# Causal attention of a two-layer block: value products on quarters of the TensorE array, score products on quarter rows two heads at a time, and other weights for its place beside the grouped attention

## The chip, the cores and the metric

The kernel runs on one core of a Trainium2 chip. The metric is the device time of one execution in microseconds, the median of three runs. Engines: TensorE (PE; PEld is its weight load), VectorE (DVE), ScalarE (ACT), GpSimd (POOL), SyncE (SP, which issues transfers).

## What is computed

Eight batch elements of 512 rows and 128 channels pass through two layers, each modulated by a small table. Layer 0: linear attention with 16 heads and an MLP (`attn0`), then 8 dense experts with a SiLU gate (`experts`). Layer 1: causal softmax attention with 8 heads of 16 channels (`attn1`), then a grouped attention with 16 heads of 64 channels, whose values are mixed and whose outputs are masked by top-2 gates over 8 experts (`gates`, `values`, `heads`). The change is in the causal attention. The reference in short, its shapes scaled up by the input (8 elements, T = 512, H = 8, HD = 16):

```python
qkv = (x @ Wqkv).reshape(b, t, 3, H, HD)
q, k, v = ...
scores = einsum('bhqd,bhkd->bhqk', q, k) * scale
scores = scores + head_scales * geo_bias
scores = where(causal, scores, -inf)
attn = softmax(scores, axis=-1)
out = einsum('bhqk,bhkd->bhqd', attn, v)
return out.reshape(b, t, d) @ Wout
```

The geometric bias is folded into the query weights once, in the setup.

## The kernel before, in words

Everything is float32 and lies in SBUF for one element at a time; matmul results go to eight PSUM banks of 512 columns: F0 to F3 for everything but the grouped attention, S0, S1 (scores), TB and OB for that one. Each engine has its own program, written as generators per stage that wait on semaphores. A stage's generator yields marks. `schedule` takes a list of main marks and a list of marks beside them, and runs the second evenly among the first, by weight: `weight(name, m)` is 1 for most marks, and for the marks of the causal attention it was (i+1)/4, with i the query tile. All engines follow the same order of marks, so it fixes each queue.

The steady loop, for element b: `heads(b-1)`, 83 steps of the grouped attention of the element before, with `attn1(b)`, `gates(b)`, and of the next element `load`, `attn0` and `moe_in` beside them; then `experts(b+1)` with the end of `heads(b-1)` and `values(b)` beside them. Element 0's causal attention has nothing beside it. Element 7's is beside `heads(6)`, with its gates and 24 marks of its values behind it.

The causal attention of an element (`attn1`): ScalarE copies the queries, transposed (channel by row), to `q1T` (a name for `attT`); the keys, transposed, go to `k1T`; `k1z[:, h, :]` is `k1T` with all channels but those of head h set to zero, made for heads 0 to 3 by ScalarE (L1142) and for heads 4 to 7 by GpSimd (L690). Then 32 head steps n = 8 i + h over query tile i (128 rows) and head h. The key width is w = 128 (i+1).
- TensorE, at mark n: the score of n (L892: the contraction over all 128 channels, of which 16 count) and the causal mask by a bf16 matmul on top (L893), in F0 or F2 by turns; the transposes of the probabilities of n-2 into F3 (L740); the value product of n-3 (L908), for each key tile with the transposed probabilities as the weights and 17 columns of `v1` (16 channels and a column of ones, which gives the denominator) streaming.
- VectorE: the negated maximum of n (L1451); after each query tile a copy of F1 to `o1` (L1445).
- ScalarE: the copy of the transposed probabilities of n-2 to `p1T` (L1149), the exponential of n (L1155).
`p1`, `p1T` and `nmax1` have two buffers each. At the end the division (L1456, L1458), a transpose and the output projection (L919).

The grouped attention in `steps`: score pairs on the two row halves (L1023), maximum (L1571), exponential (L1240), transposes (L740) and their copy (L1227), value products on the two column halves (L1060); `queries`, `back`, `mixed` and `result` are further kinds of step (L1014, L1027 with L1565, L1035, L1041).

## Time and profile before

| | us |
|---|---|
| median of three runs | 2946.02 |
| lowest and highest | 2940.43, 2952.31 |
| the profiled execution | 2954.08 |
| its span, first to last instruction | 2952.4 |
| TensorE busy | 2493.8 |
| VectorE busy | 1553.8 |
| ScalarE busy | 1360.1 |
| GpSimd busy | 803.0 |
| mean granted TensorE clock | 0.932 |

The rows further down are from the profiled execution, and so are all durations. One turn of the steady loop is some 350 us. Matmul records show how long one takes from first column to last result, and they overlap: the pace is read from when the next one starts.

### The profile page before, as it was taken

The numbers are of one execution on the slowest core, as the hardware profiler recorded it, in microseconds if no ns is written. First come the engines' busy times: TensorE is split into PE (matmuls) and PEld (weight loads), VectorE is DVE, ScalarE is ACT, GpSimd is POOL, SyncE is SP. The second block draws the span as 40 slices with busy tenths as digits, with TensorE's granted clock in tenths as the row PEclk, the third lists the DMA queues.
The fourth block names the chain that finished last, engine by engine and source line by source line (L and its number), as shares of the span: only waits on it lengthen the run. The fifth ranks groups of instructions, "written<-read, shape, count | busy, mean of one in ns | idle before, by whom it ended". The sixth has DMA issues, their size and how long they took to land.

```text
span 2952.4 us, 41528 instructions
## 1 busy us (share of the span) xinstructions
PE 2493.8 (84%) x15660; PEld 1540.7 (52%) x15660; DVE 1553.8 (53%) x2640; ACT 1360.1 (46%) x2923; POOL 803.0 (27%) x376
## 2 busy tenths in 40 slices
PE   4886799889897898978988898978989789886787
PEld 2354346554475445654466544754456544664455
DVE  3224683456635475364844457354753648446732
ACT  0232236463364625555265633646255552653364
POOL 0000560015600183012800147001740129004500
PEclk7887799999999999999999999999999999997799
DMA  2110110202010030101201121010301012000101
GB/s 77 39 55 1 29 44 1 58 15 69 22 29 31 15 87 4 44 15 47 58 1 44 30 58 33 11 49 15 80 12 44 15 43 62 1 15 18 37 23 40
DMA packets 210688, 101.15 MB, mean 34 GB/s; under 512 B 137367, under 2 KB 189620, under 8 KB 210492
## 3 DMA queue, kind: packets, MB, share of 16 engines
q1 hardware_dynamic: 205052, 95.74, 11.7%
q10 hardware_dynamic: 5440, 2.75, 0.3%
q8 instruction: 128, 2.10, 0.3%
q14 instruction: 68, 0.56, 0.1%
HBM read 77.48 MB, written 20.99 MB: 33 GB/s over the span
## 4 chain that ended last, share of the span: by engine, by line
PE 54%; ACT 10%; DVE 9%; issue 9%; POOL 4%; DMA 0%; DVEq 0%; POOLq 0%; ACTq 0%
PE bank L740 11%; PE bank L1023 10%; PE bank L1060 7%; PE bank L892 4%; POOL prod L725 4%; PE bank L855 3%; PE bank L852 3%; PE bank L908 3%; PE bank L860 3%; ACT pr L1240 3%; ACT prT L1227 3%; DVE prod L1524 2%; PE bank L1035 2%; PE bank L1014 2%; DVE nmax L1571 1%
## 5 line engine op out<-in xcount | busy, mean ns | idle before, releaser
L725 POOL TENSOR_TENSOR prod<-pv,mixv 128x1024 f32<-128x1024 f32 x190 | 609.8, 3253 | 251.3 <-ACT pv L1187 173.6
L1571 DVE TENSOR_REDUCE nmax<-bank 128x1 f32<-128x512 f32 x512 | 340.9, 686 | 541.0 <-PE bank L1023 540.6
L1227 ACT ACTIVATE prT<-bank 128x512 f32<-128x512 f32 x512 | 305.7, 597 | 609.9 <-PE bank L740 605.7
L1023 PE MATMUL bank<-keys,qs 64*128 64x512 f32 x896 | 278.4, 695 | 184.7 <-ACT pr L1240 67.2
L664 POOL TENSOR_TENSOR rstd<-vareps,minus_half 128x4 f32<-128x4 f32 x48 | 48.4, 1009 | 1272.2 <-DVE vareps L1334 1272.2
L1240 ACT ACTIVATE pr<-bank,nmax 128x512 f32<-128x512 f32 x512 | 350.3, 686 | 68.2 <-DVE nmax L1571 66.9
L740 PEld LDWEIGHTS bank<-ident,pr 128*128 128x128 f32 x2048 | 240.1, 149 | 265.5 <-issue 252.6
L740 PE MATMUL bank<-ident,pr 128*128 128x128 f32 x2048 | 347.0, 296 | 33.4 <-ACT prT L1227 32.5
L1127 ACT ACTIVATE arena<-bank 128x512 f32<-128x512 f32 x256 | 152.9, 597 | 473.8 <-PE bank L852 425.9
L1060 PE MATMUL bank<-prT,vals 128*64 128x128 f32 x3584 | 264.9, 293 | 51.4 <-ACT prT L1227 51.4
L1532 DVE TENSOR_REDUCE vals<-prod 128x128 f32<-128x1024 f32 x224 | 269.1, 1208 | 41.9 <-POOL prod L725 41.9
L1423 DVE TENSOR_TENSOR arena<-bank,arena 128x512 f32<-128x512 f32 x256 | 174.9, 685 | 214.8 <-PE bank L855 191.7
L855 PE MATMUL bank<-h1T,Wu 128*128 128x512 f32 x512 | 268.6, 607 | 20.1 <-DVE arena L1423 20.1
L1451 DVE TENSOR_REDUCE nmax<-bank 128x1 f32<-128x128 f32 (+3 forms) x256 | 125.8, 492 | 289.1 <-PE bank L893 288.5
L852 PE MATMUL bank<-h1T,Wg 128*128 128x512 f32 x512 | 267.1, 603 | 2.2 <-ACT h1T L1092 2.2
L860 PE MATMUL bank<-arena,Wd 128*128 128x512 f32 x512 | 263.7, 600 | 2.8 <-DVE arena L1423 2.3
L1060 PEld LDWEIGHTS bank<-prT,vals 128*64 128x64 f32 x3584 | 209.3, 146 | 97.0 <-issue 69.3
L892 PE MATMUL bank<-arena,attT 128*128 128x512 f32 (+3 forms) x512 | 202.1, 480 | 4.7 <-ACT arena L1155 3.2
L1023 PEld LDWEIGHTS bank<-keys,qs 64*128 64x128 f32 x896 | 76.1, 196 | 237.0 <-issue 103.1
L1524 DVE TENSOR_TENSOR prod<-pv,mixv 128x1024 f32<-128x1024 f32 x66 | 181.6, 2752 | 0.0
L855 PEld LDWEIGHTS bank<-h1T,Wu 128*128 128x128 f32 x512 | 97.6, 193 | 149.9 <-issue 112.2
L1149 ACT ACTIVATE arena<-bank 128x128 f32<-128x128 f32 (+3 forms) x256 | 112.1, 438 | 124.2 <-PE bank L740 123.4
(231 smaller groups left out, 3272.7 us busy)
## 6 DMA issues: line engine op xcount, KB each, us to landing
Wg<-in_L_ffn_Wg SPq DMA_DIRECT2D x64, 256.0 KB, 2.7
Wu<-in_L_ffn_Wu SPq DMA_DIRECT2D x64, 256.0 KB, 3.1
Wd<-in_L_ffn_Wd SPq DMA_DIRECT2D x64, 256.0 KB, 3.7
out_rows<-on SPq DMA_DIRECT2D x32, 512.0 KB, 2.6
onR<-out_rows SPq DMA_DIRECT2D x32, 512.0 KB, 3.8
xin<-in_L_attn_x SPq DMA_DIRECT2D x8, 256.0 KB, 4.3
mask_rows<-masko SPq DMA_DIRECT2D x8, 256.0 KB, 4.3
maskR<-mask_rows SPq DMA_DIRECT2D x8, 256.0 KB, 6.8
```

Source lines behind the costliest of these rows:

```text
L725: g.tensor_tensor(*value_piece(n), ALU.mult).then_inc(vprod_r[0], 1)
L740: last = pe.transpose(dst[:, i * P:(i + 1) * P], src(i), ident[:, :])
L852: pe.matmul(F0[:, :], Wg[:, e % 2, j * P:(j + 1) * P], hbT[:, :], start=True, stop=True).then_inc(gu_g[0], 1)
L855: pe.matmul((F2, F3)[n % 2][:, :], Wu[:, e % 2, j * P:(j + 1) * P], hbT[:, :], start=True, stop=True).then_inc(gu_u[0], 1)
L860: pe.matmul(F1[:, :], Wd[:, e % 2, j, :], act[:, m % 3, :], start=(m == 0), stop=(m == n_all - 1)).then_inc(down_ps[0], 1)
L892: pe.matmul(f[:, 0:w], q1T[:, i * P:(i + 1) * P], k1z[:, h, 0:w], start=True, stop=False, skip_group_check=True)
L1023: pe.matmul(S[(turn + odd) % len(S)][:, :], qs[half, j % 3, r, :], keys[half, p, :], start=True, stop=True).then_inc(s_ps[0], 1)
L1060: last = pe.matmul(OB[DS * odd:DS * odd + DS, at:at + P], vals[:, j, h - 1 + odd, :], prT[:, (m - 1 + odd) % 3, j * P:(j + 1) * P], start= ...
L1227: s.activation(prT[:, m % 3, :], TP[m % len(TP)][:, :], ACT.Copy).then_inc(pT_r[0], 1)
L1240: s.activation(pr[:, x % NPR, :], bank_k[:, :], ACT.Exp, bias=nmax[:, x % NPR:x % NPR + 1], accum_out=den[:, i % 2, h:h + 1]).then_inc(s_o ...
L1532: v.tensor_reduce(vals[:, i, HQ * q:HQ * q + HQ, :], prod[:, m % NPROD, :].rearrange("p (h d e) -> p h d e", h=HQ, e=NE), X_AXIS, ALU.add) ...
L1571: v.tensor_reduce(nmax[:, m % NPR:m % NPR + 1], S[turn % len(S)][:, :], X_AXIS, ALU.max, negate=True).then_inc(nmax_r[0], 1)
```

## The change

- **Keys.** `k1z` has two tiles instead of eight: the keys times `parity`, whose column 0 is one on the channels of even heads and column 1 on those of odd heads (made once in the setup). VectorE writes both from PSUM. `k1T`, and the masking on ScalarE and GpSimd, are gone.
- **Scores.** A head's score contracts only over the 32 channels (partitions) of its pair of heads, of which `parity` leaves 16. Heads are taken in `ORDER1`, so that two successive ones lie on different 32 partitions, and both scores are issued one behind the other at even n, into F0 and F2, then both masks.
- **Maxima and exponentials.** VectorE does both maxima of such a pair at the even mark, ScalarE both exponentials. `p1` and `nmax1` have four buffers.
- **Values.** Four heads together (`QUAD`): `v1`, padded with zeros to 32 columns per head (`DV`), is the weight, and the transposed probabilities stream, 128 columns each. The four outputs lie on the four quarters of the partitions of F1, transposed. `p1T` has six buffers. ScalarE copies them to `o1T` once per query tile, TensorE transposes them back, VectorE copies to `o1`.
- **Marks.** `attn1` has two more (37 head marks, not 35), and their weight is (i+2)/4, not (i+1)/4. In the steady loop 32 of the 83 steps of `heads` now stand beside the head marks, where 25 did: steps 7 to 38, where it was 8 to 32.

Order on TensorE, last query tile of element 1, beside the heads of element 0 (bank0, 2, 3 and 1 are F0, F2, F3 and F1; bank4 to 7 are the grouped attention's). Before:

```order
L892 MATMUL bank2<-arena,attT 128x512
L893 MATMUL bank2<-causal_bf,ident_bf 128x128
L740 MATMUL bank3<-ident,arena 128x128 x4
L908 MATMUL bank1<-v1,arena 128x17 x4
L1023 MATMUL bank5<-keys,qs 128x512
L1023 MATMUL bank4<-keys,qs 128x512
L740 MATMUL bank6<-ident,pr 128x128 x4
L892 MATMUL bank0<-arena,attT 128x512
L893 MATMUL bank0<-causal_bf,ident_bf 128x128
L740 MATMUL bank3<-ident,arena 128x128 x4
L908 MATMUL bank1<-v1,arena 128x17 x4
```

Now, with L896 the score, L898 the mask, L744 the transposes, L916 the values, L1036, L1073 and L1048 the grouped attention's:

```order
L896 MATMUL bank0<-arena,attT 128x512
L896 MATMUL bank2<-arena,attT 128x512
L898 MATMUL bank0<-causal_bf,ident_bf 128x128
L898 MATMUL bank2<-causal_bf,ident_bf 128x128
L744 MATMUL bank3<-ident,arena 128x128 x4
L916 MATMUL bank1<-arena,v1 32x128 x16
L1073 MATMUL bank7<-prT,vals 64x128 x8
L744 MATMUL bank3<-ident,arena 128x128 x4
L1048 MATMUL bank5<-spread,onR 64x32 x32
L744 MATMUL bank6<-ident,pr 128x128 x4
L744 MATMUL bank3<-ident,arena 128x128 x4
```

The two scores moved together, and the value products of four heads stand in one place, sixteen for four key tiles.

Order on ScalarE at the same place. Before:

```order
L1149 ACTIVATE arena<-bank3 128x512
L1155 ACTIVATE arena<-bank0,nmax1 128x512
L1227 ACTIVATE prT<-bank6 128x512
L1232 ACTIVATE qs<-bank4 128x512
L1149 ACTIVATE arena<-bank3 128x512
L1155 ACTIVATE arena<-bank2,nmax1 128x512
```

Now (L1164 the copy, L1170 the exponential, L1157 the copy to `o1T`):

```order
L1164 ACTIVATE arena<-bank3 128x512
L1170 ACTIVATE arena<-bank0,nmax1 128x512
L1170 ACTIVATE arena<-bank2,nmax1 128x512
L1238 ACTIVATE oaT<-bank7 128x256
L1242 ACTIVATE prT<-bank6 128x512 x2
L1255 ACTIVATE pr,den<-bank4,nmax 128x512
L1157 ACTIVATE o1T<-bank1 128x256
L1164 ACTIVATE arena<-bank3 128x512
```

The exponential of the odd head moved up beside that of the even one, and the next score pair on TensorE waits for it.

The diff, cut to its core:

```diff
-E1 = A1 + N1 + 3
+E1 = A1 + N1 + 5
+ORDER1 = (0, 2, 1, 3, 4, 6, 5, 7)
+QUAD = 4
+DV = 32
+NPT = 6
...
-    return (1 + min((m - A1 - 1) // H1, NT - 1)) / NT if name == "attn1" and A1 < m <= E1 else ...
+    return (2 + min((m - A1 - 1) // H1, NT - 1)) / NT if name == "attn1" and A1 < m <= E1 else ...
...
-        k1z = part(0, [H1, T])
-        v1 = sb("v1", [P, NT, H1, D1 + 1])
-        nmax1 = sb("nmax1", [P, 2])
-        p1 = part(4096, [2, T])
-        p1T = part(5120, [2, T])
+        k1z = part(0, [2, T])
+        v1 = sb("v1", [P, NT, H1, DV])
+        o1T = sb("o1T", [P, 2 * P])
+        nmax1 = sb("nmax1", [P, 4])
+        p1 = part(1024, [4, T])
+        p1T = part(3072, [NPT, T])
...
 # TensorE
-                for n in range(N1 + 3):
-                    if n < N1:
-                        i, h = n // H1, n % H1
+                wait(pe, k1_r, b, 2)
+                for n in range(N1 + 5):
+                    if n < N1 and n % 2 == 0:
+                        i = n // H1
                         w = (i + 1) * P
-                        f = (F0, F2)[n % 2]
-                        if i == 0:
-                            wait(pe, k1z_r[h // (H1 // 2)], b, h % (H1 // 2) + 1)
-                        if n >= 2:
-                            wait(pe, p1_r, b, n - 1)
-                        pe.matmul(f[:, 0:w], q1T[:, i * P:(i + 1) * P], k1z[:, h, 0:w], ...)
-                        pe.matmul(f[:, w - P:w], ident_bf[:, :], causal_bf[:, :], ...).then_inc(s1_ps[0], 1)
+                        wait(pe, p1_r, b, n)
+                        for odd, f in enumerate((F0, F2)):
+                            h = ORDER1[n % H1 + odd]
+                            rows = slice(h // 2 * 2 * D1, h // 2 * 2 * D1 + 2 * D1)
+                            pe.matmul(f[:, 0:w], q1T[rows, i * P:(i + 1) * P], k1z[rows, h % 2, 0:w], ...)
+                        for f in (F0, F2):
+                            pe.matmul(f[:, w - P:w], ident_bf[:, :], causal_bf[:, :], ...).then_inc(s1_ps[0], 1)
...
-                    if n >= 3:
+                    if 3 <= n <= N1 + 2 and n % QUAD == (QUAD + 2) % QUAD:
                         m = n - 3
-                        i, h = m // H1, m % H1
-                        if h == 0 and i >= 1:
+                        i, half = m // H1, m % H1 // QUAD
+                        if half == 0 and i >= 1:
                             wait(pe, o1_r, b, i)
                         wait(pe, p1T_r, b, m + 1)
                         for j in range(i + 1):
-                            last = pe.matmul(F1[:, h * (D1 + 1):(h + 1) * (D1 + 1)], p1T[:, m % 2, j * P:(j + 1) * P], v1[:, j, h, :], ...)
+                            for k in range(QUAD):
+                                h = ORDER1[QUAD * half + k]
+                                c = h % QUAD * DV
+                                last = pe.matmul(F1[c:c + DV, half * P:(half + 1) * P], v1[:, j, h, :], p1T[:, (m - QUAD + 1 + k) % NPT, j * P:(j + 1) * P], ...)
+                        last.then_inc(o1T_ps[0], 1)
+                    if n >= H1 + 4 and n % H1 == 4:
+                        i = n // H1 - 1
+                        wait(pe, o1T_r, b, i + 1)
+                        for half in range(2):
+                            last = pe.transpose(F1[:, (2 + half) * P:(3 + half) * P], o1T[:, half * P:(half + 1) * P], ident[:, :])
+                        last.then_inc(o1_ps[0], 1)
...
 # ScalarE
+                        s.activation(o1T[:, :], F1[:, 0:2 * P], ACT.Copy).then_inc(o1T_r[0], 1)
...
+                    for m in (n, n + 1) if n < N1 and n % 2 == 0 else ():
+                        wait(s, nmax1_r, b, m + 1)
+                        s.activation(p1[:, m % 4, 0:w], (F0, F2)[m % 2][:, 0:w], ACT.Exp, bias=...)
...
 # VectorE
-                v.tensor_copy(k1T, F2[:, :]).then_inc(k1_r[0], 1)
+                for odd in range(2):
+                    v.tensor_scalar(k1z[:, odd, :], F2[:, :], parity[:, odd:odd + 1], None, ALU.mult).then_inc(k1_r[0], 1)
```

## Rows read from the trace of the kernel before

**Rows 1.** The page, part 1: busy us (share of the span) xinstructions.
```profile
PE 2493.8 (84%) x15660; PEld 1540.7 (52%) x15660; DVE 1553.8 (53%) x2640; ACT 1360.1 (46%) x2923; POOL 803.0 (27%) x376
```

**Rows 2.** Stretch, its us, busy us (count) of PE, PEld, DVE, ACT, POOL; clock, DMA.
```profile
426.00:449.00 23.00, 16.12 (x101) 9.76 (x101) 8.34 (x23) 13.56 (x27) 5.13 (x6) 0.93 0.00 1
449.00:537.00 88.00, 84.43 (x672) 63.63 (x673) 32.74 (x62) 54.68 (x132) 0.33 (x1) 0.98 0.13 37
537.00:673.00 136.00, 105.71 (x863) 68.48 (x859) 69.62 (x161) 72.81 (x155) 15.59 (x12) 0.91 0.06 17
673.00:774.00 101.00, 96.89 (x323) 45.50 (x324) 74.49 (x72) 30.89 (x54) 77.17 (x24) 1.00 0.25 66
```

**Rows 3.** Waits of TensorE in 537 to 673 us, total us, times, longest.
```profile
PE bank L1023 <- DVE on L1565: 6.8, 3, 3.2
PE bank L1060 <- ACT prT L1227: 6.3, 9, 0.8
```

**Rows 4.** The same view: element 0's attention, element 7's, and behind it.
```profile
196.00:251.00 55.00, 51.77 (x336) 41.37 (x336) 16.85 (x36) 31.37 (x69) 3.46 (x5) 0.91 0.09 31
...
2532.00:2620.00 88.00, 84.40 (x707) 64.24 (x707) 31.88 (x60) 54.35 (x133) 0.00 (x0) 0.98 0.05 13
2620.00:2790.00 170.00, 119.27 (x864) 75.71 (x864) 112.99 (x126) 64.12 (x150) 74.85 (x28) 0.79 0.07 21
```

**Rows 5.** Groups in 449 to 537 us: count, busy us, mean ns, idle before.
```profile
L892 PE MATMUL bank<-arena,attT 128*128 128x128 f32 (+3 forms) x64 | 24.8, 472 | 0.0
L908 PE MATMUL bank<-v,arena 128*128 128x17 f32 x160 | 20.2, 248 | 0.0
L1240 ACT ACTIVATE pr<-bank,nmax 128x512 f32<-128x512 f32 x20 | 13.7, 686 | 0.0
```

**Rows 6.** Timeline of TensorE, 509 to 517 us: start, duration, what.
```profile
509.64 1.12 PE L892 MATMUL bank<-arena,attT 128*128 128x512 f32 x2
510.60 0.22 PE L893 MATMUL bank<-causal_bf,ident_bf 128*128 128x128 bf16 x1
510.65 0.60 PE L740 MATMUL bank<-ident,arena 128*128 128x128 f32 x4
511.10 0.96 PE L908 MATMUL bank<-v,arena 128*128 128x17 f32 x8
511.99 1.13 PE L1023 MATMUL bank<-keys,qs 64*128 64x512 f32 x4
513.05 0.65 PE L740 MATMUL bank<-ident,pr 128*128 128x128 f32 x4
513.54 1.02 PE L892 MATMUL bank<-arena,attT 128*128 128x512 f32 x2
514.40 0.22 PE L893 MATMUL bank<-causal_bf,ident_bf 128*128 128x128 bf16 x1
...
515.79 1.09 PE L1060 MATMUL bank<-prT,vals 128*64 128x128 f32 x16
516.82 0.70 PE L892 MATMUL bank<-arena,attT 128*128 128x512 f32 x1
```

**Rows 7.** Groups over the span: masked keys, and a copy of 128x256.
```profile
L1223 ACT ACTIVATE oaT<-bank 128x256 f32<-128x256 f32 x128 | 49.2, 385 | 12.9 <-PE bank L1060 12.6
L690 POOL TENSOR_TENSOR arena<-att,head_of 128x512 f32<-128x512 f32 x32 | 32.2, 1039 | 52.8 <-DVE att L1439 52.8
L1142 ACT ACTIVATE arena<-att,head_of 128x512 f32<-128x512 f32 x32 | 20.4, 710 | 0.0
```

**Rows 8.** Timeline of element 0's attention, last query tile.
```profile
244.42 0.68 ACT L1155 ACTIVATE arena<-bank,nmax 128x512 f32<-128x512 f32 x1
...
245.48 0.22 PE L893 MATMUL bank<-causal_bf,ident_bf 128*128 128x128 bf16 x1
245.74 0.69 DVE L1451 TENSOR_REDUCE nmax<-bank 128x1 f32<-128x512 f32 x1 [1.56 <-PE bank L893]
...
246.68 0.68 ACT L1155 ACTIVATE arena<-bank,nmax 128x512 f32<-128x512 f32 x1
```

More of the change, by code:

```diff
@@ L116, in weight @@
 def weight(name, m):
-    return (1 + min((m - A1 - 1) // H1, NT - 1)) / NT if name == "attn1" and A1 < m <= E1 else FINISH_SHARE if name == "finish" else 1
+    return (2 + min((m - A1 - 1) // H1, NT - 1)) / NT if name == "attn1" and A1 < m <= E1 else FINISH_SHARE if name == "finish" else 1
 def mark_of(k):
@@ L148, in build @@
         head_of16 = sb("head_of16", [P, H1])
+        parity = sb("parity", [P, 2])
         ones_row = sb("ones_row", [1, P])
@@ L368, in build @@
         p1T_r = sem("p1T_r", N1)
+        o1T_ps = sem("o1T_ps", 2 * NT)
+        o1T_r = sem("o1T_r", NT)
         o1_ps = sem("o1_ps", NT)
@@ L635, in _ @@
             g.memset(v1[:, :, :, D1:D1 + 1], 1.0)
+            g.memset(v1[:, :, :, D1 + 1:DV], 0.0)
             for e in range(NE):
@@ L687, in attn1 @@
                 yield 5
-                wait(g, k1_r, b, 1)
-                for h in range(H1 // 2, H1):
-                    g.tensor_tensor(k1z[:, h, :], k1T, head_of16[:, h:h + 1].to_broadcast([P, T]), ALU.mult).then_inc(k1z_r[1][0], 1)
                 wait(g, rows1a_in, b, 16)
@@ L1138, in attn1 @@
                 s.activation(v1[:, :, :, 0:D1], F3[:, :].rearrange("p (i h d) -> p i h d", i=NT, h=H1), ACT.Copy).then_inc(v1_r[0], 1)
-                wait(s, k1_r, b, 1)
-                for h in range(H1 // 2):
-                    s.activation(k1z[:, h, :], k1T, ACT.Copy, scale=head_of16[:, h:h + 1]).then_inc(k1z_r[0][0], 1)
                 yield A1
-                for n in range(N1 + 2):
-                    if n >= 2:
+                for n in range(N1 + 4):
+                    if n >= H1 + 3 and n % H1 == 3:
+                        i = n // H1 - 1
+                        wait(s, o1T_ps, b, 2 * i + 2)
+                        s.activation(o1T[:, :], F1[:, 0:2 * P], ACT.Copy).then_inc(o1T_r[0], 1)
+                    if 2 <= n <= N1 + 1:
                         m = n - 2
@@ L1321, in _ @@
             floor_gate(rtab[:, 2:5, :], rsgn, rabs, k)
+            v.tensor_reduce(parity[:, :], head_of16[:, :].rearrange("p (g o) -> p o g", o=2), X_AXIS, ALU.add)
             v.memset(nmax1[:, :], 0.0).then_inc(setup_done[0], 1)
```

49 lines of the change are left out of this document (23 added, 26 removed).

## The prediction

> **What bounds the kernel now.** I read the page's busy shares first: TensorE is busy 84% of the span, no other engine above 53% [rows 1]. A share averages stages with different limits, so the next view is the busy time by stretch, for one turn of the steady loop [rows 2]. Of 348 us, 23 go by ahead of the causal attention (TensorE 70% busy), 88 beside it (96%, ScalarE 62%), 136 behind it (78%), 101 in the experts (96%). The reader is to see that TensorE is the limit where the changed code runs, and that the 136 us behind it keep 30 us idle. The longest waits there are the grouped attention's own: its scores wait for a score bank that DVE still reads, its values for ACT's copy [rows 3]. Beside the causal attention 84.4 of 88 us are busy. Element 0 has its attention alone, 55 us with TensorE 94% busy, and element 7 runs 88 us beside the heads and 170 us behind them at 70% [rows 4].
>
> **TensorE's work on attn1, per element.** The groups of lines in the 88 us show the 64 score and 160 value passes [rows 5], the timeline the pace [rows 6]. A float32 matmul is two passes. Four transposes of 128 columns take 510.65 to 511.10, so 0.11 us for 128 columns; the two passes of a 512-column score take 513.54 to 514.40, 0.43 each, the same rate. Hence:
> - Scores: 16 passes at each width of 1, 2, 3, 4 tiles: 160 tiles of 128 columns, 160 x 0.1075 = 17.2 us.
> - Values: 160 passes, eight of them 511.10 to 511.99, 0.111 each: 17.8 us. They stream 17 columns and are paced by loading 128 columns of weights.
> - Transposes of ten key tiles for eight heads, 80 x 0.11 = 8.8, one mask per head, 32 x 0.055 (510.60 to 510.65) = 1.8: unchanged. In all 45.6 us, and 88 - 45.6 = 42.4 us are the 25 steps of the heads stage beside them, 1.7 us each.
>
> After the change two score matmuls lie on different rows of the array and four value matmuls on different columns. No row of before shows quarters, but two show halves. Four 512-column passes on half the rows (L1023) take 511.99 to 513.05, 1.06 us, where two matmuls one after the other would be 1.72. Sixteen passes on half the columns (L1060) take 515.79 to 516.82, 1.03 us: eight slots of 0.11 = 0.88. So pairs do run at once, and each such stretch costs 0.15 to 0.20 us above its slots; the score behind L1060 takes 0.96 (509.64 to 510.60) instead of 0.86, another 0.1. I take 0.25 us for each entry into a divided array.
> - Scores: 17.2 / 2 = 8.6. Values: 20 groups of four heads and one key tile, two slots each, 40 x 0.11 = 4.4, if all four run at once. Entries: 16 score pairs and 8 value groups, 24 x 0.25 = 6.0. Transposes of the outputs back: 8 x 0.11 = 0.9. Together 19.9 against 35.0: **15 us less per element**.
> - Bounds of the four-at-once price: best, 0.11 us for a slot of four, as a pair now; worst, one after another, 160 x 0.11 = 17.6. I take the best, since the pairs show no loss at all. Bounds of an entry: 0.1 (only the delay behind it) to 0.35 (0.2 in it, 0.1 behind it, and 0.05 for a first load), that is 2.4 to 8.4 us.
>
> The Trainium skill ("TensorEngine Tiling (Array Packing)", Key Properties) says that changing the tiling mode drains TensorE, which speaks against a change with 24 more such visits per element. The trace agrees in kind, by the 0.15 to 0.20 above; the page gives no price, and without the rule the sum would be 6 us per element better. The Trainium skill ("TensorE: Matmul & The Clock Gate", Measured speedup vs the span model) has 2.38 times for three column tiles; an estimate of four at that 79% yield makes the values 5.6 us instead of 4.4. No run here shows it yet.
>
> **Other engines.** ACT drops four copies that mask the keys (0.71 us each [rows 7]), 2.5 us with their overlap, and gains four copies of 128x256 like L1223, 0.385 each: 1 us less. POOL drops four of 1.04. DVE makes a second 512-column operation, about 0.7, in front of the first score; it takes the place of ACT's first masked key, 0.71, so that chain is unchanged. ACT is at 62% beside the attention and DVE at 37%, TensorE's saving raises these to about 70% and 43%: they cover it. The parity vector is one small setup step: nothing. On each engine's queue the order changes in one way that counts: DVE does both maxima, ACT both exponentials, and the next score pair waits for the second exponential.
>
> **What the new weights move.** The attention gets 32 steps of the heads stage beside it, not 25; behind it are 45, not 51, ahead 6, not 7. So the 88 us stretch becomes 88 - 15 + 7 x 1.7 = 84.9; I add 1 us of waits for the second exponential: 86, **2 us gained**. Behind it 6 steps go, 10.2 us of TensorE work, but that stretch is 22% idle and also holds the next element's first attention and the gates, whose chains of norms and selections are then covered by fewer steps. Ends: 0 (chains set the time) and 10 (TensorE sets it). With TensorE at 78% neither holds alone; I take half, **5 us**. Ahead, one step fewer in a chain-bound stretch: 1 us. That makes 8 us for each of elements 1 to 6. Element 7 has the same attention (2) but a tail at 70%, with DVE busy 113 of 170 us: 3 more, 5 in all. Element 0 alone: a head pair at full width is now 2 x 2.26 us, by the exponentials at 244.42 and 246.68 [rows 8]. After, the pair is a chain: scores 1.06, from the mask's start to the maximum's 0.26 (245.48 to 245.74), two maxima 1.38, one exponential 0.68, 3.4 us. Four pairs save 4.4 us; at three tiles by the same sum 2.8, at two and one tile about 1 each; the longer way of the output back to rows costs 1. **8 us**.
>
> **Sum.** 6 x 8 + 5 + 8 = 61 us, against the profiled execution's 2954.08: 2893. The median of the three runs is 8 us below that execution, so **2885 us**, a ratio of 0.979. A difference under 0.5%, 15 us, can't be told from no change.
>
> **Rivals.**
> - *TensorE sets the time everywhere.* All 15 us arrive in each element and the steps moved cost nothing: 7 x 15 + 10 = 115 us, 2831. For it: 96% busy beside the attention. Against it: the 30 us idle behind. Chance 0.13.
> - *Only two of four column parts run at once.* Values 8.8 us instead of 4.4: 7 x 4.4 = 31 us of the gain go, 2916. For it: the trace shows two at once and never more. Against it: two cost exactly what one costs. Chance 0.11.
> - *A wait takes the place of the work.* The next pair of scores waits for the second exponential, which stands on ACT behind the grouped attention's copies and exponentials (0.69 us for an exponential). One such in the way of each of 16 pairs, less what the moved steps cover, is some 6 us: 7 x 6 = 42 us given back, 2927. For it: one score pair in flight instead of two single ones a step apart. Against it: two marks of other TensorE work lie between. Chance 0.16.
> - *Slower: the quarters go one at a time.* The four value matmuls of a tile stream 128 columns each, 17.6 us where 17.8 stood; the saving is 1.8 us, not 15. The attention stretch becomes 88 - 2 + 12 = 98, 10 us longer, the stretch behind 5 shorter and the one ahead 1: 4 x 7 = 28 us, and element 0 about 5 longer: 2979. It decides from the point where a slot of four costs above 0.31 us (12.4 us for the values). Against it: L1060's halves. Chance 0.07.
> - *The change is made but the regrouped steps do nothing measurable*, since the stretches behind keep their length and the attention's saving is eaten by the added steps: 2938 to 2950. Chance 0.05.
>
> **How the numbers follow.** The forecast has 0.48, with own range 2860 to 2910 (3 to 10 us per element where I took 8, and the entry at its bounds). The cases above it and below it leave 0.13 at 2831 and 0.39 from 2916 up. Range 2838 to 2934: it takes in the two milder rivals and part of the full gain, and leaves out the serial case, the null case, and the far end of the full gain. Faster by over 0.5% is below 2931: 0.48 + 0.13 + 0.11 + two thirds of 0.16 = 0.83. Within: the rest of 0.16 and 0.04 of the null case, 0.09. Slower: 0.07 and 0.01, 0.08.
>
> **What would show it.** Four value matmuls starting within 0.03 us of each other, the next four 0.11 later; 40 such slots. Score pairs of 512 columns in about 1.06 us. TensorE's busy time per turn down by some 15 us. The stretch with the attention at 83 to 89 us with five more heads in it, the one behind at 126 to 136. ACT's first of two exponentials without a wait between it and the second. I would be wrong if the value matmuls start 0.11 us apart one by one, if TensorE waits for ACT's exponential over 0.3 us in most pairs, if an entry costs over 0.4 us, or if the stretch behind the attention keeps its 136 us or grows. In element 0 a granted clock well below the 0.91 of before would show that the thinner stream of matmuls there runs at 1.2 instead of 2.4 GHz, and would take its 8 us back.

## The result and the profile after

| | before | after |
|---|---|---|
| median, us | 2946.02 (7 runs) | 2929.9 (7 runs) |
| lowest and highest | 2940.43, 2953.73 | 2923.28, 2935.88 |
| profiled execution | 2954.08 | 2925.12 |
| its span | 2952.4 | 2923.4 |
| TensorE busy | 2493.8 | 2399.3 |
| granted clock | 0.932 | 0.921 |

The ratio is 0.994, with a 95% interval of 0.9919 to 0.9962: 16 us faster, where 61 were forecast. The kernel before ran again beside the experiments, with medians of 2952.18 us (beside e1 to e4), 2944.85 (e5 to e8) and 2945.1 (e9 to e11); each ratio below is against its own neighbour, and a difference of two medians from different groups can be off by some 7 us. Of the page, part 1 (busy us, share of the span, instructions; compare [rows 1]):

```profile
PE 2399.3 (82%) x15724; PEld 1397.4 (48%) x15724; DVE 1530.1 (52%) x2649; ACT 1339.4 (46%) x2923; POOL 769.2 (26%) x345
```

TensorE does 94 us less and the kernel gains 16 to 29 us. The view by stretch for one turn of the loop (length, busy us and count of each engine, clock, DMA; compare [rows 2]): ahead of the causal attention, beside it, behind it, the experts.

```profile
1113.00:1140.80 27.80, 21.44 (x104) 12.30 (x102) 15.82 (x30) 11.68 (x23) 4.21 (x4) 0.88 0.00 1
1140.80:1226.10 85.30, 76.17 (x756) 49.62 (x758) 32.01 (x63) 58.17 (x146) 0.00 (x0) 0.98 0.13 38
1226.10:1359.90 133.80, 101.34 (x791) 65.77 (x783) 64.88 (x159) 70.38 (x150) 15.57 (x12) 0.89 0.06 17
1359.90:1461.30 101.40, 97.26 (x323) 45.66 (x324) 74.85 (x73) 30.31 (x52) 77.52 (x24) 1.00 0.25 66
```

TensorE had been busy 96% of the stretch beside the attention; now it is 89%. What it waits for there (total, times, longest):

```profile
PE bank L744 <- ACT arena L1164: 2.9, 4, 0.9
PE bank L1036 <- ACT pr L1255: 1.7, 2, 1.6
PE bank L1073 <- ACT prT L1242: 1.5, 3, 0.8
```

The stretch behind still has 32 us in which TensorE is idle. Its waits there, beside [rows 3]:

```profile
PE bank L1036 <- DVE on L1583: 9.8, 4, 6.8
PE bank L1036 <- ACT pr L1255: 9.3, 4, 4.2
PE bank L1073 <- ACT prT L1242: 5.8, 9, 0.8
```

The wait for DVE's division (L1583, L1565 before) grew from 6.8 us, 3.2 at most, to 9.8 us, 6.8 at most.

**The quarters cost what was forecast.** Groups in 1140.8 to 1226.1 (compare [rows 5]), then TensorE's timeline in element 0 and at a place of eight value slots (start, duration, what):

```profile
L896 PE MATMUL bank<-arena,attT 32*128 32x128 f32 (+3 forms) x64 | 12.9, 480 | 0.0
L916 PE MATMUL bank<-arena,v 128*32 128x128 f32 x156 | 5.9, 278 | 0.0
```

```profile
236.06 1.13 PE L896 MATMUL bank<-arena,attT 32*128 32x512 f32 x4 [0.54 <-ACT arena L1170]
237.12 0.28 PE L898 MATMUL bank<-causal_bf,ident_bf 128*128 128x128 bf16 x2
237.24 0.61 PE L744 MATMUL bank<-ident,arena 128*128 128x128 f32 x4
...
1213.37 1.08 PE L916 MATMUL bank<-arena,v 128*32 128x128 f32 x32
1214.38 0.44 PE L1073 MATMUL bank<-prT,vals 128*64 128x128 f32 x4
```

A pair of 512-column scores takes 1.06 us up to the mask. Thirty-two value passes take 1.01 us: eight slots of four, whose four starts lie 7 ns apart and the next slot 0.11 us on. So all four column parts run at once, and 20.2 busy us of values [rows 5] are 5.9.

For the experiments I cut each trace into stretches by TensorE's own lines: the experts' matmuls, up to the first score (pre), first score to last value matmul (attention), on to the next experts (behind). Means over elements 1 to 6 in us, the last columns for elements 0 and 7; "steps" is how many steps of `heads` stand from the first score to the last value matmul, and behind it. Each row is one profiled execution.

| kernel | steps | pre | attention | behind | el. 0 att. | el. 7 att., behind | span |
|---|---|---|---|---|---|---|---|
| before | 25, 51 | 26.2 | 85.1 | 133.7 | 54.0 | 87.8, 331.9 | 2952.4 |
| after | 30, 47 | 26.3 | 84.6 | 132.4 | 56.9 | 83.8, 317.0 | 2923.4 |
| e1_old_weights | 24, 52 | 23.7 | 81.8 | 137.2 | 64.8 | 78.8, 326.2 | 2930.2 |
| e2_before_new_weights | 31, 46 | 26.5 | 94.4 | 121.3 | 54.0 | 96.0, 310.2 | 2922.3 |
| e3_scores_full | 30, 47 | 26.4 | 89.1 | 131.8 | 54.0 | 88.8, 322.9 | 2958.1 |
| e4_filler | 30, 47 | 26.8 | 84.6 | 132.7 | 60.1 | 83.9, 317.6 | 2935.8 |
| e5_tail_unweighted | 31, 46 | 25.4 | 87.2 | 122.5 | 54.6 | 86.4, 314.8 | 2871.9 |
| e6_tail_fill2 | 31, 46 | 25.2 | 87.7 | 122.2 | 47.7 | 86.4, 314.5 | 2862.9 |
| e7_unpaired | 31, 46 | 26.1 | 95.2 | 121.9 | 71.3 | 86.1, 314.8 | 2933.5 |
| e8_before_shifted | 30, 47 | 28.5 | 93.1 | 131.4 | 55.0 | 94.1, 321.7 | 2995.6 |
| e9_swap | 30, 47 | 25.4 | 85.1 | 129.0 | 56.9 | 83.9, 320.3 | 2909.0 |
| e10_values_single | 31, 46 | 25.5 | 92.8 | 120.7 | 75.7 | 91.1, 311.3 | 2918.7 |
| e11_fill2_w3 | 35, 42 | 26.9 | 89.2 | 117.9 | 48.4 | 92.0, 316.3 | 2867.3 |

### The profile page after: what moved, and what is told of

Read it like the earlier page. It is cut to its first block, busy times and chain, and to the rows that moved or that the text cites. A ratio compares the mean times of both kernels' runs of the same rounds, so it can differ in the third digit from the quotient of the medians.

```text
span 2923.4 us, 41764 instructions
## 1 busy us (share of the span) xinstructions
PE 2399.3 (82%) x15724; PEld 1397.4 (48%) x15724; DVE 1530.1 (52%) x2649; ACT 1339.4 (46%) x2923; POOL 769.2 (26%) x345
## 4 chain that ended last, share of the span: by engine, by line
PE 49%; ACT 11%; DVE 10%; issue 10%; POOL 6%; DMA 0%; ACTq 0%; DVEq 0%; POOLq 0%
PE bank L1036 10%; PE bank L744 10%; PE bank L1073 7%; POOL prod L729 5%; ACT prT L1242 3%; ACT pr L1255 3%; PE bank L856 3%; PE bank L859 3%; PE bank L864 3%; PE bank L896 2%; DVE prod L1542 2%; PE bank L1027 2%; PE bank L1048 2%; DVE nmax L1589 2%; PE bank L916 1%
## 5 line engine op out<-in xcount | busy, mean ns | idle before, releaser
L1242 ACT ACTIVATE prT<-bank 128x512 f32<-128x512 f32 x512 | 306.6, 599 | 602.1 <-PE bank L744 599.0
L1036 PE MATMUL bank<-keys,qs 64*128 64x512 f32 x896 | 285.2, 711 | 208.9 <-ACT pr L1255 92.8
L671 POOL TENSOR_TENSOR rstd<-vareps,minus_half 128x4 f32<-128x4 f32 x48 | 48.4, 1009 | 1367.1 <-DVE vareps L1350 1367.1
L744 PE MATMUL bank<-ident,pr 128*128 128x128 f32 x2048 | 351.1, 298 | 30.6 <-ACT prT L1242 29.7
L744 PEld LDWEIGHTS bank<-ident,pr 128*128 128x128 f32 x2048 | 241.4, 150 | 270.5 <-issue 259.4
L1073 PE MATMUL bank<-prT,vals 128*64 128x128 f32 x3584 | 262.1, 291 | 55.1 <-ACT prT L1242 55.1
L1073 PEld LDWEIGHTS bank<-prT,vals 128*64 128x64 f32 x3584 | 207.3, 145 | 117.9 <-issue 83.0
L1469 DVE TENSOR_REDUCE nmax<-bank 128x1 f32<-128x128 f32 (+3 forms) x256 | 113.8, 485 | 227.3 <-PE bank L898 227.3
L1036 PEld LDWEIGHTS bank<-keys,qs 64*128 64x128 f32 x896 | 76.8, 198 | 262.9 <-issue 111.9
L1542 DVE TENSOR_TENSOR prod<-pv,mixv 128x1024 f32<-128x1024 f32 x66 | 189.3, 2869 | 0.0
L864 PEld LDWEIGHTS bank<-arena,Wd 128*128 128x128 f32 x512 | 97.1, 191 | 132.0 <-issue 117.3
L1164 ACT ACTIVATE arena<-bank 128x128 f32<-128x128 f32 (+3 forms) x256 | 113.3, 442 | 91.6 <-PE bank L744 89.0
```

Of the source, the lines that this page charges most:

```text
L744: last = pe.transpose(dst[:, i * P:(i + 1) * P], src(i), ident[:, :])
L864: pe.matmul(F1[:, :], Wd[:, e % 2, j, :], act[:, m % 3, :], start=(m == 0), stop=(m == n_all - 1)).then_inc(down_ps[0], 1)
L1036: pe.matmul(S[(turn + odd) % len(S)][:, :], qs[half, j % 3, r, :], keys[half, p, :], start=True, stop=True).then_inc(s_ps[0], 1)
L1073: last = pe.matmul(OB[DS * odd:DS * odd + DS, at:at + P], vals[:, j, h - 1 + odd, :], prT[:, (m - 1 + odd) % 3, j * P:(j + 1) * P], start= ...
L1242: s.activation(prT[:, m % 3, :], TP[m % len(TP)][:, :], ACT.Copy).then_inc(pT_r[0], 1)
L1542: v.tensor_tensor(*value_piece(n), ALU.mult).then_inc(vprod_v[0], 1)
```

## The experiments

### The weights taken apart from the attention

**e1_old_weights**: the changed kernel with the step weights of before.

```diff
-    return (2 + min((m - A1 - 1) // H1, NT - 1)) / NT if name == "attn1" and A1 < m <= E1 else ...
+    return (1 + min((m - A1 - 1) // H1, NT - 1)) / NT if name == "attn1" and A1 < m <= E1 else ...
```

> The changed kernel with the old weights (i+1)/4, so 25 or 26 steps of the grouped attention beside the causal attention and not 32. Theory A (the stretch behind the causal attention is set by its chains of small operations, so steps taken from it save nothing, while each step put beside the attention costs about 1.4 us): the attention stretch of elements 1 to 6 falls from 84.6 to about 76 us, the one behind rises from 132.4 by at most 2, median about 2885. Theory B (the stretch behind is set by TensorE's work, and the new weights were needed): the attention stretch falls to about 80 because TensorE then waits for the exponentials, the one behind rises to 140, median 2935 or more.

Measured: 2931.39 us (11 runs), ratio 0.9928 [0.9904, 0.9952], the same as the change itself. Theory A's 76 and 2885 us fail; theory B's 80, 140 and 2935 come near (81.8, 137.2, 2931.39). The new attention alone takes only 3.3 us off its stretch and the one behind is 3.5 us longer than before. Five steps more behind than in the change make that stretch 4.8 us longer, 1.0 each.

**e2_before_new_weights**: the kernel before, with the new weights alone (the same line the other way round).

> The kernel before with the new weights (i+2)/4 alone. Theory A: the attention stretch rises from 85.1 to about 95 us, the one behind falls from 133.7 to about 132, median about 2995. Theory B: the one behind falls by about what the attention gains, 10 us, and the median stays near 2946.

Measured: 2919.42 us (6 runs), 0.9895 [0.9867, 0.9923]. The weights alone give 27 us against the first seven runs of the kernel before, 33 against those beside it, more than the whole change. Six steps more beside the attention cost 9.3 us, 1.6 each, near the 1.7 of the prediction. Five fewer behind it save 12.4 us, where theory A had 2 and theory B 10; B's equal median did not come. That is 2.5 us a step, where the prediction had 0.8, but it is not the price of a step: the weights also move every later mark against the steps. One turn, attention and behind:

```profile
1138.50:1233.00 94.50, 90.59 (x762) 68.01 (x764) 34.87 (x65) 59.22 (x145) 0.00 (x0) 1.00 0.12 35
1233.00:1354.50 121.50, 95.22 (x769) 62.79 (x769) 65.13 (x157) 69.78 (x148) 15.61 (x12) 0.92 0.06 18
```

So the riddle was where the gain of the attention went. The stretch behind has 47 steps in the change and 46 here, yet is 11.1 us longer.

### Which small chain meets which step

Each engine works through its queue in the order of the marks, so what stands ahead of a step in a queue delays it. The change has two marks more at the end of `attn1`, with weights of 1.25: the weights of the steady loop's list sum to 88.25, in e2 to 85.75. That shifts every later mark against the steps. In the change step 49 of `heads`, the fourth back division, meets (has scheduled right beside it) the second mark of the next element's first attention; in e2 it meets the third of the gates. TensorE, then VectorE in the changed kernel at that place:

```profile
1257.07 0.60 PE L744 MATMUL bank<-ident,pr 128*128 128x128 f32 x4
1264.42 2.08 PE L1036 MATMUL bank<-keys,qs 64*128 64x512 f32 x4 [6.75 <-DVE on L1583]
```

```profile
1257.75 0.28 DVE L1347 BATCH_NORM_AGGREGATE mv<-stats 128x2 f32<-128x6 f32 x3
1258.06 0.17 DVE L1350 TENSOR_SCALAR vareps<-mv 128x4 f32<-128x4 f32 x1
1259.35 1.11 DVE L1355 TENSOR_SCALAR nrm_o<-xin,mv,rstd 128x128 f32<-128x128 f32 x4 [1.12 <-POOL rstd L671]
1260.50 0.69 DVE L1367 TENSOR_TENSOR arena<-nrm_o,rows 128x512 f32<-128x512 f32 x1
...
1263.27 0.17 DVE L1350 TENSOR_SCALAR vareps<-mv 128x4 f32<-128x4 f32 x1
1263.35 0.20 DVE L1580 RECIPROCAL rden<-den 128x8 f32<-128x8 f32 x1
1263.58 0.69 DVE L1583 TENSOR_TENSOR on<-bank,rden 128x512 f32<-128x512 f32 x1
```

The division waits in VectorE's queue for a norm, a round trip to GpSimd, a modulation and a second norm's statistics, and TensorE waits 6.75 us for the division. Three kernels test this from three sides.

**e5_tail_unweighted**: the change, with the last two head marks weighing nothing.

```diff
+    if name == "attn1" and E1 - 2 < m <= E1:
+        return 0
```

> The changed kernel with weight 0 for its two added marks, so that every mark behind the attention stands beside the same step of the heads as in the kernel before with the new weights, whose stretch behind takes 121.3 us where the change has 132.4. Theory C (the length of the stretch behind is set by which small chain on VectorE or ScalarE stands ahead of which step of the heads, and the change's two extra marks moved them): the stretch behind falls to 121 to 125 us, the attention stays at 84 to 87, the median falls from 2930 to about 2865. Theory D (the new attention itself, by its lower clock or its longer way of the output, makes the stretch behind longer): the stretch stays near 132, the median near 2930.

Measured: 2882.87 us (5 runs), 0.9793 [0.9774, 0.9812]. The stretch behind falls from 132.4 to 122.5, as theory C has it, and D fails. This edit of two weights gains 47 us on the changed kernel, three times what the change had gained.

**e8_before_shifted**: the old attention (e2), with 2.5 marks of weight added behind it, so that its later marks stand where the change has them.

```diff
+    if name == "attn1" and m == E1 + 1:
+        return 3.5
```

> The kernel before with the new weights and 2.5 more weight on the first mark behind the attention's steps, so that all marks from the gates on stand beside the same steps of the heads as in the change, two steps of the heads standing between with nothing beside them. Theory C: the stretch behind grows from 121.3 to about 132 us and the median from 2919 to about 2985, the attention itself being untouched. Theory D: it grows by the one step alone, to 124, and the median to about 2935.

Measured: 2983.65 us (5 runs), 1.0151 [1.0128, 1.0174], 64 us slower than e2. The stretch behind goes from 121.3 to 131.4 without any new attention, theory C's number again, and the wait of 6.8 us is there too (L1025, L1062 are the grouped scores and values, L1567 the division, L1242 the exponential):

```profile
PE bank L1025 <- ACT pr L1242: 9.3, 4, 4.2
PE bank L1025 <- DVE on L1567: 8.8, 4, 6.8
PE bank L1062 <- ACT prT L1229: 5.8, 9, 0.8
```

**e9_swap**: the change, with one pair of marks exchanged, so that the division meets the gates' mark; all weights as they are.

```diff
+                k = both.index(("gates", (b, offset), [3]))
+                assert both[k - 1] == ("attn0", (b, offset + 1), [2])
+                both[k - 1:k + 1] = [both[k], both[k - 1]]
```

> The changed kernel, with two of the marks beside the attention over heads exchanged: the gates' third mark now goes ahead of the latent attention's second mark, so that the step of the fourth back division (step 49) meets a small mark of the gates, as it does in the two kernels whose stretch behind took 121 to 122 us, and no longer the normalisation of the latents. Nothing else moves and no weight changes. If it is that meeting that holds TensorE (in the changed kernel it waits 6.75 us at L1036 for the fourth back division, against 4.97 us at most where the gates' mark meets it), the stretch behind goes from 132.4 us to 126 to 129 us in each of elements 0 to 6, and the whole to about 2895 to 2910 us. The rival is that the meeting is one among many: the wait then moves to the next step, which meets the normalisation now, the stretch keeps its 131 to 133 us and the whole its 2925 to 2935 us. The attention's stretch stays at 84 to 85 us by both.

Measured: 2904.68 us (4 runs), 0.9864 [0.984, 0.9887]; behind 129.0. In the stretch of one turn the long wait is gone, and part of it stands elsewhere (L1039 the grouped scores, L1586 the division, L747 the transposes, L1358 the norm):

```profile
PE bank L1039 <- ACT pr L1258: 9.3, 4, 4.2
PE bank L1076 <- ACT prT L1245: 5.8, 9, 0.8
PE bank L1039 <- DVE on L1586: 4.6, 4, 1.6
PE bank L747 <- DVE nrm_o L1358: 4.0, 1, 4.0
```

TensorE waits 5.2 us less for the divisions, and now 4.0 us for the norm itself. Both theories hold in part: this meeting is 3.4 of the 10 us. The other 6 come with the shift of all later marks and with the one step more; those were not taken apart mark by mark.

The waits are only half of it. In the stretch behind, means over elements 1 to 6 in us:

| kernel | steps | TensorE busy | idle | at the half clock |
|---|---|---|---|---|
| before | 51 | 104.1 | 29.6 | 17.4 |
| after | 47 | 99.8 | 32.6 | 27.3 |
| e1_old_weights | 52 | 107.6 | 29.6 | 26.1 |
| e2_before_new_weights | 46 | 95.0 | 26.3 | 19.3 |
| e5_tail_unweighted | 46 | 95.1 | 27.4 | 19.9 |
| e8_before_shifted | 47 | 100.0 | 31.5 | 28.4 |
| e9_swap | 47 | 98.6 | 30.4 | 20.5 |
| e11_fill2_w3 | 42 | 92.1 | 25.8 | 20.5 |

Between e5 and the change lie 9.9 us: 5.2 us idle and 4.7 us of longer busy time, of which the one step more is a part. After the wait of 6.75 us in the change the granted clock was 0.50 from 1264.4 to 1270.4 us, and the four score passes at 1264.42 took 2.08 us, where the same ones take 1.13 at 1253.15. So a long wait was paid twice there. The old attention shows the same in e8, so the lower clock of this stretch doesn't come from the new one.

### What the new attention is worth

**e8 against the change** is also the cleanest pair for the attention: same steps, same weights, same meetings. One turn, the attention's stretch in e8:

```profile
1159.10:1252.10 93.00, 88.68 (x754) 67.12 (x752) 33.56 (x63) 58.66 (x143) 0.00 (x0) 1.00 0.12 35
```

Against 85.30 us with 76.17 busy: 12.5 us less work, 4.8 us more waiting, 7.7 us less time. Over elements 1 to 6 the means are 13.4 less work (88.8 to 75.4 busy), 4.8 more waiting and 8.5 less time. By medians the new attention gains 54 us there (2983.65 to 2929.9), and 37 where the meetings are good (e2 to e5), or 55 and 29 when each is set against the kernel before run beside it.

**e3_scores_full**: the change, with each score contracting over all 128 rows.

```diff
-                            rows = slice(h // 2 * 2 * D1, h // 2 * 2 * D1 + 2 * D1)
+                            rows = slice(0, P)
```

> The changed kernel with each score contracted over all 128 channels again, the pair still issued together; the scores then mix the heads of one parity. If TensorE's work sets the attention stretch, four passes one after the other instead of two at a time, less the saved entries, add about 5 us per element: the stretch goes from 84.6 to about 89, median about 2965. If waits for exponentials and maxima set it, the stretch and the median (2930) stay.

Measured: 2950.1 us (10 runs), 1.0008 [0.9989, 1.0028]. The attention's stretch grows by 4.5 us. The prediction's own terms give 4.6: 8.6 us of scores that no longer run in pairs, less 16 entries at 0.25. For the scores the price arrives in full. Element 0's attention gets 2.9 us shorter, for which the section on its clock has the reason, and the median stays 15 us below the 2965 forecast.

**e10_values_single**: e5, with the values one head at a time.

```diff
-                            for k in range(QUAD):
-                                ...
-                                last = pe.matmul(F1[c:c + DV, half * P:(half + 1) * P], v1[:, j, h, :], p1T[:, (m - QUAD + 1 + k) % NPT, j * P:(j + 1) * P], ...)
+                            last = pe.matmul(F1[:, h * (D1 + 1):(h + 1) * (D1 + 1)], p1T[:, m % NPT, j * P:(j + 1) * P], v1[:, j, h, 0:D1 + 1], ...)
```

> The kernel whose last two attention steps weigh nothing (2882.87 us, attention stretch 87.2 us per element), with the values' product as it was before the change: one head at a time over the full array, 17 columns of values streaming under 128 columns of loaded weights, result straight into the place it had, no transposes back and no copy on ScalarE. By the rows, the values then cost TensorE 17.8 us per element in place of 4.4, and 0.9 us of back transposes and about 2 us of waits at the row's end go away: 10.5 us more work. If TensorE's work still sets the attention's stretch, it takes 96 to 98 us per element and the whole goes to 2955 to 2965 us. If a part of what the quarter-column values save only turned into waits for the exponentials (TensorE waits about 10 us of this stretch in the changed kernel), the stretch takes 89 to 93 us and the whole comes to 2900 to 2930 us. The stretch behind stays at 121 to 124 us by both.

Measured: 2919.37 us (5 runs), 0.991 [0.9891, 0.9929]; attention 92.8 against 87.2. The two stretches, first e10, then e5:

```profile
1153.20:1245.90 92.70, 87.15 (x761) 64.36 (x762) 33.33 (x65) 58.35 (x145) 0.00 (x0) 0.98 0.12 35
```

```profile
1121.20:1209.40 88.20, 79.59 (x764) 51.27 (x766) 33.29 (x65) 58.65 (x148) 0.00 (x0) 0.96 0.12 37
```

The values' work is 7.6 us more, where 10.5 was expected, and the waits are 3.1 us fewer: the waiting theory's number. Forty per cent of the work that the quarter columns save turns into waits in this turn, 36 per cent by the means over elements 1 to 6 (8.7 us of work, 3.1 of waits). That the median fits too is partly luck: element 0's attention grew from 54.6 to 75.7 us, which the theory did not price.

**e7_unpaired**: e5, with maxima and exponentials one per mark again.

```diff
-                    for m in (n, n + 1) if n < N1 and n % 2 == 0 else ():
+                    for m in (n,) if n < N1 else ():
```

(The same edit in ScalarE's and in VectorE's program.)

> As the run with the two marks unweighted, but VectorE's maximum and ScalarE's exponential of the odd head stand at the odd mark again, TensorE as in the change. If the pairing puts waits in the way of the grouped attention's steps on DVE and ACT, the attention stretch falls below 84 us, by up to 5. If the pairing helps by having the exponentials early, the stretch grows by 2 to 6 us, since the next score pair waits for the odd head's exponential.

Measured: 2935.43 us (12 runs), 0.997 [0.9958, 0.9981]; the attention's stretch is 95.2 against 87.2, with a wait that the paired kernel has not (L898 is the score there, L1172 the exponential):

```profile
PE bank L898 <- ACT arena L1172: 9.1, 11, 1.7
```

Without the pairing of both engines' steps the score pairs would have lost all that they gain: 8.0 us per element, 16.7 in element 0 (with the granted clock there at 0.64 instead of 0.73, so not all of it is the waits).

### Element 0's clock

By tens of microseconds from 195 to 245 in the changed kernel:

```profile
195.00:205.00 10.00, 7.62 (x45) 4.00 (x45) 2.48 (x10) 5.15 (x17) 0.00 (x0) 0.66 0.00 0
205.00:215.00 10.00, 9.46 (x55) 4.76 (x55) 2.79 (x8) 4.92 (x16) 0.00 (x0) 0.50 0.00 0
215.00:225.00 10.00, 9.25 (x48) 4.25 (x44) 2.04 (x4) 4.51 (x11) 0.00 (x0) 0.50 0.01 2
225.00:235.00 10.00, 9.08 (x58) 4.83 (x56) 3.38 (x7) 4.49 (x10) 0.00 (x0) 0.63 0.00 0
235.00:245.00 10.00, 8.02 (x67) 4.30 (x67) 3.39 (x7) 6.13 (x12) 0.00 (x0) 1.00 0.01 2
```

TensorE runs at 1.2 GHz for 20 us while it is busy over 90% of the time; before, the same stretch was at 2.4 GHz from 215 us on. The clock falls in both kernels, after a few microseconds in which TensorE is less than half busy: before at 200.5 us (2.96 of the 6.8 us ahead busy), in the change at 198.2 (1.64 of 3.4). What differs is how long it stays down, 10 us against 34. The same instructions also fill more of the time at the half clock, so the 90% is in part its effect. The stretch at the half clock in the kernel before, in the change, and in e10, where it goes on to the end of the attention:

```profile
200.50:210.80 10.30, 10.30 (x48) 8.66 (x47) 2.60 (x8) 4.70 (x16) 0.00 (x0) 0.50 0.48 159
198.20:232.30 34.10, 31.82 (x175) 15.96 (x175) 8.68 (x22) 15.66 (x43) 0.00 (x0) 0.50 0.00 0
199.80:240.00 40.20, 39.28 (x175) 29.95 (x176) 8.35 (x22) 14.91 (x40) 0.00 (x0) 0.50 0.00 0
```

Element 0's attention is the same program in the change, e1, e5 and e9, as nothing stands beside it; it took 56.9, 64.8, 54.6 and 56.9 us, at granted clocks of 0.68, 0.54, 0.73 and 0.68. So it varies by 10 us between executions, with the clock.

**e4_filler**: six matmuls of 128 columns over the full array ahead of each pair of scores, in element 0 alone, into a bank that nobody reads there.

```diff
+                        for _ in range(3 if b == (0, 0) else 0):
+                            pe.matmul(OB[:, 0:P], ident[:, :], block8[:, :], start=True, stop=True)
+                            pe.matmul(OB[:, P:2 * P], ident[:, :], block8[:, :], start=True, stop=True)
```

> The changed kernel with six extra float32 matmuls of 128 columns into an unused bank ahead of each score pair of element 0 only, whose attention stretch shows a granted clock of 0.67 and takes 57 us. If the half clock is what takes the gain of element 0 away, the granted clock rises above 0.9 there and the stretch falls to about 50 us in spite of 21 us of added matmuls. Rival, the chain of maxima and exponentials sets it at either clock: the stretch stays at 57 or grows.

Measured: 2935.9 us (10 runs), 0.9949 [0.9932, 0.9967]. The clock is 1.00 from 205 us on, but the stretch takes 60.1 us, the rival's side of 57. The fillers were too many to decide: TensorE is busy for 53.4 us of it, with 21 us of fillers by the expectation's count. So e6 has two.

**e6_tail_fill2**: e5 with two fillers.

```diff
+                        for _ in range(2 if b == (0, 0) else 0):
+                            pe.matmul(OB[:, 0:P], ident[:, :], block8[:, :], start=True, stop=True)
```

> As the run with the two marks unweighted, and two extra float32 matmuls of 128 columns ahead of each score pair of element 0. If the half clock (0.50 from 205 to 225 us) costs element 0 its gain: granted clock above 0.9, element 0's attention 49 to 52 us, 5 us or more less than without. If the chain of maxima and exponentials sets it at either clock: 56 us or more.

Measured: **2868.46 us** (4 runs), 0.9742 [0.9727, 0.9757], the fastest of all, by a hair (e11 has 2869.19). The slowest of its four runs, 2868.79, is below the fastest of e5's five, 2873.68. Element 0's attention takes 47.7 us against 54.6 in e5:

```profile
195.00:205.00 10.00, 8.30 (x75) 5.52 (x73) 2.98 (x10) 5.76 (x21) 0.00 (x0) 1.00 0.00 0
205.00:215.00 10.00, 8.96 (x87) 5.55 (x87) 3.76 (x9) 5.45 (x16) 0.00 (x0) 1.00 0.01 2
215.00:225.00 10.00, 8.88 (x81) 5.88 (x80) 3.54 (x7) 6.32 (x15) 0.00 (x0) 1.00 0.01 2
```

In e3, whose scores use all 128 rows while the values stay on quarters, the clock stays at 1.00 too, with TensorE less busy than in the change:

```profile
205.00:215.00 10.00, 7.84 (x63) 5.05 (x62) 3.23 (x9) 5.70 (x17) 0.00 (x0) 1.00 0.00 0
215.00:225.00 10.00, 7.94 (x52) 4.53 (x51) 3.27 (x7) 5.04 (x13) 0.00 (x0) 1.00 0.01 2
```

Set side by side, e3 and e10 tell which product the low clock goes with. Element 0's granted clock was 0.91 with both products on the full array (before), 0.99 with the values alone on quarters (e3), 0.53 with the scores alone on quarter rows (e10), 0.68 with both (the change). It goes with the score pairs on quarter rows, not with the value products, in one execution of each; why, no run here shows.

### More of the same weight

**e11_fill2_w3**: e6 with (i+3)/4.

```diff
-    return (2 + min((m - A1 - 1) // H1, NT - 1)) / NT if name == "attn1" and A1 < m <= E1 else ...
+    return (3 + min((m - A1 - 1) // H1, NT - 1)) / NT if name == "attn1" and A1 < m <= E1 else ...
```

> The kernel with two filler matmuls in element 0 and the last two steps without weight (2868.46 us), with attention step weights of (3+i)/4 of a mark in place of (2+i)/4: the total of the weights is 94.5, and four to five more steps over the heads go beside the attention, four to five fewer behind it. At the prices that the exchange of weights alone has shown in the kernel before (1.9 us per step beside the attention, 2.5 us per step behind it) the attention's stretch goes from 87.7 to about 96 us and the stretch behind from 122.2 to about 111 us: 3 us less per element, about 2848 us in the whole. If the meeting of the small chains with the steps over the heads (which shifts by four to five) counts for more than the number of steps, the stretch behind takes 118 us or more and the whole is 2870 to 2910 us.

Measured: 2869.19 us (5 runs), 0.9751 [0.9726, 0.9775], no different from e6. The attention's 96 us, the 111 behind and the 2848 of the first theory fail; the stretch behind (117.9) and the whole stand at the lower edge of the second's (118 and 2870). Four steps more beside the attention cost 1.5 us, 0.4 each: TensorE's busy time grows by 2.1 us, where four steps at 1.7 would be 6.8, and its idle time falls by 0.6, with the granted clock at 1.00 where it was 0.97; the rest is not taken apart. Four fewer behind save 4.3, 1.1 each. Elements 1 to 6 gain 2 us each, by the sum of their four stretches, and element 7 is 12 us longer (27.1, 92.0 and 316.3 against 22.8, 86.4 and 314.5). A price per step holds only for the schedule in which it was read.

## Why the prediction was right and wrong

**TensorE's work: right.** Forecast 15 us less per element; at equal steps it is 13.4 over elements 1 to 6 (e8 to the change), 12.5 in the turn shown. The slot of four at 0.11 us is confirmed, and with it the rival of two column parts falls; so does the one of one quarter at a time. The Trainium skill ("TensorE: Matmul & The Clock Gate", Measured speedup vs the span model) has 2.38 times for three column tiles of 512 columns, 79% of three; here 32 passes of 128 columns take 1.01 us for 3.5 us one by one (32 x 0.11), 3.5 times with the entry in it, so the measurement decides for the full rate.

**The attention's stretch: the term of waits was mis-sized.** "88 - 15 + 7 x 1.7 = 84.9; I add 1 us of waits": measured 84.6 for 85.1 before, with five steps more up to the last value matmul; the seven were counted to the last mark, behind it. By that count the sum gives 85.1 - 15 + 8.5 = 78.6, six less than came. Nearly all of it is waits: TensorE's idle time in this stretch was 3.4 us before and is 9.1 now, where the sum had 1 us. The rival of the waits had 6 us and their kind nearly right, but blamed the second exponential: L896 has no such row above, and e7 shows that the pairing prevents it. The waits that came are for the copies of transposed probabilities and for the grouped attention's chain. e10 shows the size of the effect: a third or more of the work saved turned into waits.

**"Behind it 6 steps go ... I take half, 5 us": this step failed.** It came to 1.3 us (133.7 to 132.4). The term priced the number of steps alone, and the two added marks were costed at nothing. TensorE's busy time did fall there, by 4.2 us, but its idle time grew by 3.0. The marks moved small chains ahead of steps on VectorE's and ScalarE's queues: without their weight the same kernel takes 122.5 us behind (e5), and their weight makes the old attention's stretch 10.1 us longer (e8); one step more is in both differences. The exchange of one pair of marks gives 3.4 us back (e9). The number of steps was priced about right: e1 and e11 show 1.0 and 1.1 us each, the forecast had 0.8, and e2's 2.5 has meetings in it. The upper end of 10 us is none either: with five steps fewer, e2 saves 12.4 and e5 11.2. The prediction named the sign, that the stretch "keeps its 136 us", and said that chains "are then covered by fewer steps", but never asked which mark each step meets, though the order of the two kernels shows it. (Its 136 is element 1's; elements 1 to 6 have 133.7.)

**Element 0: the wrong sign.** Forecast 8 us gained, measured 2.9 lost (54.0 to 56.9). The pair takes 3.6 us at full clock, near the 3.4 forecast, but the half clock, which the prediction named as what "would take its 8 us back", did that: the granted clock was 0.68, where it had been 0.91. With the clock held up it is 47.7 (e6), 6.3 us gained. The prediction had it as a sign of being wrong, with no term and no chance.

**Element 7: the gain was in the tail.** Forecast 5 us; attention and stretch behind it are 18.9 us shorter. In e2 they are 13.5 shorter, so much of it is the weights' work again. No run takes this tail apart; it made up 14 us for what the other elements missed, which is luck. The profiled difference of 29.0 us is, from element 1's first score to element 7's, 6 x 1.8; from there 18.9; element 0's attention -2.9; and 2.4 saved ahead of that attention and between it and element 1's first score.

**The ledger by medians.** Weights alone -27 (e2); the new attention under good meetings -37 (e5 less e2); the two marks' weight +47 (change less e5). That is -16. With each median set against the kernel before that ran beside it, the same three are -33, -29 and +46. By either count the expected gain was there, 62 to 64 us where 61 were forecast, and the marks that came with it gave most of it back. That the size agrees is luck. By the prediction's own terms the weights alone lose 7 x 1.7 - 5 - 1 = 6 us per element and the new attention gains 14. The runs show the weights alone gaining 2.9 from one first score to the next (e2), and the new attention 6.9 (e2 to e5).

Open: why the profiled executions differ by 29 us and the medians by 16 (before's lies 8 above its median, after's 5 below), which meetings beyond the one exchanged make up the other 6 us, and why the clock stays low beside quarter-row scores.

## What to carry to other kernels

Where a scheduler spreads one list of marks over another by weight, every added mark or changed weight moves all later ones: list which short chain stands ahead of which step on each queue, before costing the edit. Two marks of weight 1.25 decided 47 us here, a whole new attention 37 to 54. A piece of work made cheaper on the bounding engine pays until the others' chains take over: with 12.5 us of work gone, 7.7 us of time came. And don't take a price per step from one exchange of weights: it read 2.5 us in e2 and 1.0 to 1.1 in e1 and e11, as the meetings moved with the steps.

## What the hardware showed unexpectedly

- Four float32 matmuls on the four column quarters cost a slot of 0.11 us, the same as one: no loss over two halves.
- TensorE stayed at 1.2 GHz for 34 us while 93% busy, with its scores on quarter rows (98% busy for 40 us in e10, whose values use the full array); two full-array matmuls of 128 columns for each pair of scores (e6), or scores over all 128 rows (e3), kept it at 2.4 GHz. These are observations of single executions, not a threshold.
- A wait was paid twice: 6.75 us idle, then a granted clock of 0.50 from 1264.4 to 1270.4 us, in which four passes took 2.08 us instead of 1.13.
- ScalarE's change between exponential and the other function's table costs 1.28 us each way. In the change at 1324 to 1331 us, inside TensorE's longest wait for an exponential (4.2 us):

```profile
1326.99 1.28 ACT L1125 ACT_TABLE_LOAD   x1
1328.29 0.69 ACT L1125 ACTIVATE arena<-bank,cols 128x512 f32<-128x512 f32 x1
1328.99 1.28 ACT L1255 ACT_TABLE_LOAD   x1
1330.29 0.69 ACT L1255 ACTIVATE pr<-bank,nmax 128x512 f32<-128x512 f32 x1
```
